# Requesting the next group's images before the token stores, and a layer's mixing weights inside a main loop

## What is computed

```python
h = layer_norm(x @ fc0_w + fc0_b, ln0_g, ln0_b)        # embed: 3 -> 32 channels
for i in range(4):                                     # four layers
    x_ft = rfft2(h)                                    # per image and channel
    out_ft[:, :, :12, :12]  = einsum('bixy,ioxy->boxy', x_ft[:, :, :12, :12],  w1[i])   # "mix"
    out_ft[:, :, -12:, :12] = einsum('bixy,ioxy->boxy', x_ft[:, :, -12:, :12], w2[i])
    x1 = irfft2(out_ft)
    x2 = einsum('bchw,oc->bohw', h, conv_w[i]) + conv_b[i]
    h  = layer_norm(x1 + x2, ln_g[i], ln_b[i]);  h = gelu(h) if i < 3 else h
h = gelu(h @ fc1_w + fc1_b);  h = gelu(h @ fc2_w + fc2_b);  tokens = (h @ fc3_w + fc3_b)[..., 0]
```

## Time and profile before

| what | value |
|---|---|
| median of three runs | 4879.39 us |
| the profiled execution's own time | 4884.81 us |
| its span in the trace | 4883.0 us |
| TensorE matmul busy | 3992.8 us (82%) |
| VectorE / ScalarE / GpSimd busy | 48% / 43% / 17% |
| mean granted TensorE clock over the span | 0.909 of full speed |
| SyncE's queue | 182.84 MB, 12.8% of 16 DMA engines' span |

### The profile page before, as it was taken

How to read it: one execution, slowest core, us unless ns; L and a number is a source line. 1 busy time by engine, 2 the same in 40 slices (tenths; PEclk the granted TensorE clock), 3 DMA queues, 4 the chain that set the end, 5 groups by cost and what they waited for, 6 DMA issues and landing times. The chain is left out here.

```text
span 4883.0 us, 102255 instructions
## 1 busy us (share of the span) xinstructions
PE 3992.8 (82%) x39344; PEld 3051.8 (62%) x39344; DVE 2321.4 (48%) x5028; ACT 2100.9 (43%) x3178; POOL 809.0 (17%) x540
## 2 busy tenths in 40 slices
PE   0189999996899999868999999699999995867268
PEld 0068788842687878427888783278888732753146
DVE  6554444531544445225444442244445422777666
ACT  1154444465544444654454446544444473221113
POOL 0031221310212112112121221112212210000020
PEclk9989999998899999989999999799999997778679
DMA  9501202200022021000210210002112101000000
GB/s 205 162 22 60 79 21 64 75 1 16 21 71 69 21 76 63 1 16 21 79 60 21 79 60 2 15 21 79 60 28 72 60 2 31 1 1 1 0 1 9
DMA packets 168694, 213.38 MB, mean 44 GB/s; under 512 B 156402, under 2 KB 158679, under 8 KB 159874
## 3 DMA queue, kind: packets, MB, share of 16 engines
q1 hardware_dynamic: 166514, 182.84, 12.8%
q10 hardware_dynamic: 1680, 23.60, 2.0%
HBM read 147.28 MB, written 59.12 MB: 42 GB/s over the span
## 5 line engine op out<-in xcount | busy, mean ns | idle before, releaser
L765 POOL TENSOR_TENSOR rstd<-var,mhalf 128x16 f32<-128x16 f32 x240 | 698.4, 2910 | 38.8 <-POOL var L762 17.1
L742 ACT ACTIVATE h<-tp,gb 128x512 f32<-128x512 f32 x640 | 554.0, 868 | 303.9 <-PE tp L465 301.9
L708 DVE TENSOR_REDUCE ssum<-sq 128x16 f32<-128x512 f32 x640 | 432.6, 683 | 453.7 <-ACT sq L730 451.3
L762 POOL TENSOR_TENSOR var<-ssum,eps 128x16 f32<-128x16 f32 x240 | 52.0, 217 | 3146.9 <-DVE ssum L708 3146.9
L457 PEld LDWEIGHTS main<-convw,h 128*128 128x128 f32 x3072 | 416.1, 213 | 164.8 <-issue 164.8
L465 PE MATMUL tp<-ident,xn 128*128 128x128 f32 x2560 | 438.7, 299 | 85.5 <-DVE xn L699 80.8
L730 ACT ACTIVATE sq<-main 128x512 f32<-128x512 f32 x480 | 286.4, 599 | 464.0 <-PE main L457 417.4
L506 PE MATMUL main<-fwd_w,pix 128*128 128x96 f32 x4096 | 464.8, 276 | 7.0 <-ACT pix L598 7.0
L506 PEld LDWEIGHTS main<-fwd_w,pix 128*128 128x128 f32 x4096 | 459.8, 192 | 10.3 <-DVE pix L598 8.7
L457 PE MATMUL main<-convw,h 128*128 (+1 forms) x3072 | 465.6, 304 | 0.0
L465 PEld LDWEIGHTS tp<-ident,xn 128*128 128x128 f32 x2560 | 324.1, 154 | 179.6 <-DVE xn L699 141.8
(11 more groups left out here) (240 smaller groups left out, 5952.5 us busy)
## 6 DMA issues: line engine op xcount, KB each, us to landing
mixw<-mix_scratch SPq DMA_DIRECT2D x16, 4608.0 KB, 18.0
y_scratch<-t_w SPq DMA_DIRECT2D x256, 144.0 KB
yd<-y_scratch SPq DMA_DIRECT2D x32, 1152.0 KB, 7.3
mix_scratch<-mixw SPq DMA_DIRECT2D x64, 288.0 KB, 4.8
mixw<-mix_scratch ACTq DMA_DIRECT2D x1, 4608.0 KB, 13.8
h<-in_L_tok_w1r ACTq DMA_DIRECT2D x6, 576.0 KB, 9.7
h<-in_L_tok_w1i ACTq DMA_DIRECT2D x6, 576.0 KB, 10.1
h<-in_L_tok_w2r ACTq DMA_DIRECT2D x6, 576.0 KB, 18.6
```

What stands on the lines that cost most here:

```text
L708: dve.tensor_reduce(ssum[:, c % 4, :], sq[:, c % 2, :].rearrange("p (n c) -> p n c", c=CH), AX.X, ALU.add).then_inc(red_done, 1)
L742: act.activation(out, in_, fn, bias=gb[:, 1, stage:stage + 1] if l is None else gb[:, 1, bass.ds(stage, 1)], scale=gb[:, 0, stage:stage + ...
L765: pool.tensor_tensor(rstd[:, c % 4, :], var[:, c % 4, :], mhalf[:, :], ALU.pow).then_inc(rstd_done, 2)
```

## The change

Only SyncE's program is changed. No transfer is altered in shape; one is dropped.

- **Images.** The requests for a group's images and embedding weights stood at the start of the group's pass, behind the token stores of the group before. Now those of group 0 stand ahead of the loop over groups, without the wait on `main_full`; those of group `g + 1` stand right behind the layers of group `g`, after a wait until TensorE has written the last chunk of the group's last main loop. Behind them come the first layer's mixing weights for the next group, and then the token stores.
- **Mixing weights of a layer.** The request for layer `l + 1` stood at the start of pass `l`, right behind the spectrum of the stage before. Now it waits until TensorE has written eight of the sixteen chunks (`NCH // 2`) of unit 0's main loop of that pass.
- **The last group** is written out behind the loop and requests neither images nor mixing weights; before, it loaded the first layer's mixing weights once more, which nobody read.

```diff
-                with sp.Fori(0, GROUPS) as g:
-
-                    sp.wait_ge(main_full, g * CHUNKS_GROUP + START)
-                    for u in range(UNITS):
-                        sp_x(sp, g, u)
+
+                def layers(g):
                     for u in range(UNITS):
                         sp_spectrum(sp, g, 0, u, None)
                     with sp.Fori(0, LAYERS - 1) as l:
                         for u in range(UNITS):
                             if u == 0:
+                                sp.wait_ge(main_full, base_of(g, 1, 0, l)[0] + NCH // 2)
                                 sp_mixw(sp, l + 1)
                             sp_spectrum(sp, g, 1, u, l)
+                    sp.wait_ge(main_full, g * CHUNKS_GROUP + (START + CHUNKS_GROUP))
+
+                for u in range(UNITS):
+                    sp_x(sp, 0, u)
+                with sp.Fori(0, GROUPS - 1) as g:
+                    layers(g)
+                    for u in range(UNITS):
+                        sp_x(sp, g + 1, u)
                     sp_mixw(sp, 0)
                     for u in range(UNITS):
                         sp_tok(sp, g, u)
+                layers(GROUPS - 1)
+                for u in range(UNITS):
+                    sp_tok(sp, GROUPS - 1, u)
                 sp.wait_ge(tok_out, GROUPS * UNITS * TOK_DMAS * 16 + 16)
-                sp.wait_ge(mixw_in, (GROUPS * LAYERS + 1) * 16)
+                sp.wait_ge(mixw_in, GROUPS * LAYERS * 16)
```

## The result

Four runs of the changed kernel gave a median of 4808.43 us (4803.85 to 4815.36), beside 4881.36 for the kernel before in the same comparison: a ratio of 0.9849, 95% interval 0.9831 to 0.9867. The forecast was 4809 us, the range 4795 to 4826. The gain between the medians is 72.9 us, and the interval of the ratio leaves about 65 to 82. The profiled execution took 4812.15 us instead of 4884.81, 72.7 us less.

The account below looks back on a forecast made before the run. The prediction took TensorE's wait for the next group's images to bound the passages between groups. 70.1 us there plus 0.5 in the first group gave 70.6; 4879.39 less that is 4809 us, range 4795 to 4826.

Parts of the forecast that it names:

- What bounds: Between groups: TensorE's L409 wait for images, 152.2 us in four, is the largest; token stores are late next.
- The passages: At the three passages between groups, L447 starts 23.75, 23.23 and 23.09 us earlier, together 70.1 us.
- TensorE's jump: Back to the group loop's start: at most 4.9 us, so the transposes fit under the token stores and cost nothing.
- The second rival: At each passage TensorE's jump becomes the wait: at 12 us, 3.2 us lost each, 4819; chance 0.15 with added traffic.
- First group: At the start, images requested up to 5.4 us earlier are served only after the mixing weights: 0.5 us gained.
- Mixing weights: In each layer, twelve requests moved to mid main loop: worth 0, 10 us either way as ends, 40 us to spare.
- A layer's pass: In the layers, a pass changed in length by more than a microsecond or two would show the prediction wrong.
- The clock: At the passages TensorE's slow restart stays; were it gone, 3.1 us a passage, 9 us in all, giving 4800.

Follow-up runs that it names:

- e1: Changed kernel with only the images' half: a layer's mixing weights requested at the start of the pass, as before; 4810.48 us, ratio 0.9853.
- e2: Kernel before with only a layer's mixing weights moved to the middle of unit 0's main loop, images where they were; 4884.14 us, ratio 0.9998.
- e5: Kernel before with each unit's 97 rows of embedding weights requested as 96 rows and 1 row; 4824.91 us, ratio 0.9886.
- e4: Changed kernel with VectorE's and ScalarE's wait on the token stores moved to the first drain that overwrites `pix`; 4793.63 us, ratio 0.9815.
- e3: Changed kernel with the wait on `main_full` put back in front of the first group's image requests; 4810.58 us in one run.
- e9: `e7_best` with ScalarE's first request for mixing weights held until unit 0's images of the first group have landed; 4773.45 us, ratio 0.9774.
- e7_best: Changed kernel with embedding weights split into 96 rows and 1 row, and the token-store wait moved to where `pix` is overwritten; 4777.96 us, ratio 0.9791.
- e8: Changed kernel with 28 extra transposes behind unit 0's transposes of each group, filling TensorE's idle time until L447; 4820.62 us, ratio 0.9874.

## Why the prediction was right

- **What bounds.** Right. The wait of L409 fell from 152.2 to 55.5 us, and `e1` and `e2` show the images' half to be the whole gain within their intervals. What the prediction did not see is what the 24.0 us consisted of: `e5` shows most of them to be one transfer that could be made short in place, so the new order is one of two ways to shorten the same wait.
- **The passages, 70.1 us.** Measured 70.0 by the same distances. L447 comes 11.7, 11.6 and 11.6 us behind the MLP, where 11.6 were forecast. Each piece of the new chain was in the old trace: the landing of the stores (1174.70 instead of 1174.65), the table load, the copy, 0.24 to L447. That the token stores are late next was shown by taking that wait away (`e4`).
- **TensorE's jump.** Taken as 4.9 us, hence 2.7 us of slack; it is 2.70 to 2.94, and the slack in front of the table load at the first passage 4.9. The term stays at nothing. The second rival did not come true.
- **First group, 0.5 us.** The profiled executions differ by 0.2 and `e3` by 0.44. The reason given, that the images come through only once the weights are in, is borne out by `e9`, where without the weights beside them they take 9.0 us from request to transposes, in `e7_best` 18.6. The Trainium skill's page "DMA: Bandwidth & Descriptors" (section "Queues, rings and completion order") says that each DMA engine takes turns between the queues packet by packet; the packets agree, 65 small ones beside 73 large ones. Behind the images came the request of 97 rows, and it took 17.5 us from request to transposes whether or not the images were early (212.50 to 230.00; before, 213.66 to 231.14). The prediction had not seen this part of the wait; its term of 0.5 holds without it.
- **Mixing weights, 0.** Right (`e2`). Only the size of the load was off: 18.0 us from request to landing held some time behind the spectrum's load that was requested 0.6 us earlier. Where the request stands in the middle of the main loop it is 14.8 (14.9 in `e2`), and with the request left where it was, in `e1`, 17.8. That made the slack larger, 479.17 - 420.59 - 14.8 = 43.8 us instead of 40.
- **A layer's pass.** The prediction named a change of more than a microsecond or two as a sign of being wrong. By unit 0's spectrum stores the largest is 2.0 us shorter (second group, second pass, 181.25 to 179.21), others are up to 1.6 us longer; the twelve together are 2.5 us longer, no more than the spread of the runs.
- **The clock.** The slow start stayed, as said: the granted clock was 0.50 from 1174.8 to 1181.8, and the first eight L447 took 7.08, 7.09 and 5.78 us at the three passages, 5.50, 5.80 and 6.49 before. The price put on it, 3.1 us a place, was worked out for TensorE alone: that much arrived in `e8`'s first group, while at the second passage it can't be told from nothing.
- **The rest of the 72.7 us.** 70.0 and 0.2 leave 2.5 in the profiled execution. By the spectrum stores of the last layer the lead was 69.8 us, at the end of the last MLP 72.1, at the end 72.7. Differences of up to 2.7 us appear and vanish within a group at places that the change doesn't touch, in `e1` and `e2` too. I take them for the clock's dips falling on other instructions; that was not tested, and with runs of one kernel 11 us apart a difference of 2.5 can't be told from none.
- **The number.** That 4809 stands beside 4808.43 is in part luck: the sum gave 70.6 us of gain where the medians differ by 72.9, and the forecast took 4879.39 for the kernel before where the comparison has 4881.36. The two differences cancel. What the runs bear out is the mechanism and a gain of some 70 us, not the last two microseconds.

## What to carry to other kernels

A stall at the passage from one group to the next could here be priced to a microsecond from the trace before, by following the chain to what the second-latest wait releases, and counting what had been hidden under the first (here a table load of 1.28 us). Before moving a slow transfer, look at what it consists of: most of these 24 us were one request of 97 rows, and two requests in its place gained three quarters as much as the new order, and 10 us more on top of it. A wait for a store belongs in front of the instruction that overwrites, not at the start of the stage; moved there, it gave some 15 us more (`e4`).

## What was not expected of the hardware

- A load of 97 rows x 4 KB (388 KB) held TensorE 14.2 us longer than the same bytes as 96 rows and 1 row: its 97 packets started one by one over 16.3 us instead of within 1.5. 4608 KB over 128 rows landed within 14.8 us.
- 28 matmuls put ahead of TensorE's loops, where TensorE waits for its first images anyway, made the kernel some 16 us slower: the start of the layer loop then waits for issue twice (3.76 and 1.69 us) instead of once (4.29), which accounts for 10.6 of the 16.
- 5.0 us of dense matmuls before a gap of 2.1 or 1.96 us did not keep L447 from running at the lower level at the first and third passage (7.06 and 7.09 us for the first eight); 4.9 us before a gap of 1.91 did at the second (3.70).
- Beside a 4608 KB load in another queue, packets of 96 bytes got through at the pace of the load's 36 KB packets: 65 beside 73 in 6.5 us.
